# A TensorE order in which an expert tile's routing weights are spread after the down products of the tile two back

## The chip, the core and the metric

The kernel runs on one core of one Trainium2 chip. Its time is the device time of one execution in microseconds (us). The core has five engines that run their own instruction lists and meet at semaphores: TensorE (PE; its weight loads are shown as PEld), VectorE (DVE), ScalarE (ACT), GpSimd (POOL) and SyncE (SP, which only issues transfers here). An engine takes its instructions in the order in which they are written. A wait at the head of the list holds everything behind it.

## The reference, cut to what matters

Two transformer blocks over 2048 tokens of width 256. The change lies in the feed-forward part of block 0, a mixture of experts in which every expert is computed for every token, and the two best are kept by weight:

```python
scores = sigmoid(xf @ gate_w.T)                      # 8 experts
topk_w, topk_idx = top_k(scores, 2)
topk_w = topk_w / (topk_w.sum(-1, keepdims=True) + 1e-20) * 2.5
shared_out = (silu(xf @ shared_wg.T) * (xf @ shared_wu.T)) @ shared_wd.T
h = silu(einsum('td,efd->etf', xf, exp_wg)) * einsum('td,efd->etf', xf, exp_wu)
all_out = einsum('etf,edf->etd', h, exp_wd)          # 8 experts of 176 features
routed_out = (topk_w[..., None] * all_out[topk_idx]).sum(1)
x = x + attention(xn) + shared_out + routed_out
```

Block 1 has 16 causal attention heads and a dense feed-forward layer of 2048 features, whose weights come as 4-bit codes with scales. They are decoded while block 0 runs, on VectorE, ScalarE and GpSimd.

## The kernel before, in words

Tokens lie on the free axis. Block 0 takes them in G = 4 groups of 512 (loop over g). The hidden features of a group are cut into T0 = 14 tiles of 128: tiles t = 0 to 2 are the shared expert (ST = 3), tiles t = 3 to 13 hold the 8 experts' 1408 features side by side (XT = 11). The tile's number over all groups is n = 14 g + t. A product is made in single precision from a high and a low part of each operand, as three matmuls (`prod`, L415 to L417).

For each tile the steps are, with their semaphores:

- **PE `gate_up(t)`**: 12 matmuls of 512 columns into two of the four `ring` banks (s_gu). It waits for s_h of tile t-2, whose banks it takes again.
- **PE spread (L506)**, expert tiles only: one matmul of `sel` and `wT` that copies each expert's routing weights over that expert's rows, into the single bank `pv` (s_wbc). It waits for s_hw of the tile before, that is until VectorE has read `pv`.
- **PE `down0(g, t-2)`**: 6 matmuls that add the tile two back into `acc`. It waits for s_hl of that tile.
- **ACT `activate` (L893)**: SiLU of the gate bank (s_act). **DVE `gated` (L1291)**: times the up bank (s_h). **DVE routed multiply (L1377)**: times `pv` (s_hw), after a wait for s_wbc of this tile. **ACT `split_h` (L903)**: high part `hh`; in ScalarE's order it stands behind the activation of the next tile. **POOL `split_h` (L1125)**: low part `hl` (s_hl).

The order on PE is written out by hand: `gate_up(t)` with the spread at its end, then `down0(g, t-2)`, then the next group's layer norm mean behind t = 4 and its variance behind t = 7 (`ln_mean`, `ln_var`, L424 and L430).

The decoding of block 1's weights goes through the same lists. Steps k = 0 to 25 are placed at tiles n = 8 to 46, two of every three (`step_at`). Step k is, on VectorE behind the routed multiply of its tile: wait for ScalarE's `gval`, L1269, L1272 (two reads from SBUF), then L1280, L1282, L1285 that make the bits of the next value. On ScalarE behind the split of the tile before: `w4h` (L883, waits for GpSimd's `wf` of the step before) and `gval` (L886, waits for L1285 of this step). On GpSimd behind the split: `w4l` (L1125) and `wf` (L1148).

Of the kernel before, what the change touches and what calls it, by code (L numbers as in the profile page):

```python
# [84 lines left out]
def transformer_blocks(nc, xT, w0, gateT, wa, turn_w, biasc, biasv, cols, spread_c, bo, ones_c, sel_c, ident_c, identb_c,  # L85
                       mask_c, tie_c, q4, s4, x1s, w4s, out):
    ctx = ExitStack()
    with ctx:
# [224 lines left out]
        def _(sp):  # L313
# [3 lines left out]
            for n, (src, _, _) in enumerate(pieces):  # L317
                if n >= NS:
                    sp.wait_ge(s_wlo[n % 2], lo_of[n % 2].index(n - NS) + 1)
                sp.dma_start(staged(n), src).then_inc(s_stage[n % NS], 16)  # L320
                if n == 1:
                    sp.wait_ge(s_x, 16)
                    sp.dma_start(xg(1), xT[:, :, NT:2 * NT]).then_inc(s_x, 16)
# [87 lines left out]
        def _(pe):  # L411
            def prod(o, lo_hi_w, x_hi, x_lo, first, last):

                w_hi, w_lo = lo_hi_w
                pe.matmul(o, w_hi, x_hi, start=first, stop=False, skip_group_check=True)  # L415
                pe.matmul(o, w_lo, x_hi, start=False, stop=False, skip_group_check=True)  # L416
                return pe.matmul(o, w_hi, x_lo, start=False, stop=last, skip_group_check=True)  # L417

            def ln_mean(n):
                pe.wait_ge(s_x, 16 * (n + 1))  # L420
                if n > G:
                    pe.wait_ge(s_vb, 2 * (n - G))
                for k in range(KD):
                    mm = pe.matmul(ln_bank(n)[:, :], ones[:, :], xg(n)[:, k, :], start=k == 0, stop=k == KD - 1)  # L424
                mm.then_inc(s_mean, 1)

            def ln_var(n):
                pe.wait_ge(s_sq, n + 1)
                for k in range(KD):
                    mm = pe.matmul(ln_bank(n)[:, :], ones[:, :], sq[:, k, :], start=k == 0, stop=k == KD - 1)  # L430
                mm.then_inc(s_var, 1)

            def normed(n):
                pe.wait_ge(s_xl, n + 1)
                pe.wait_ge(s_xh, n + 1)

            def w(off, width, k, a, b):
                s = w0k(off, width, k, a, b)
                return wh[:, s], wl[:, s]

            def down(tile_no, off, kt, rows, last, first=False):

                pe.wait_ge(s_hl, tile_no + 1)
                th, tl = h_parts(tile_no)
                for m in range(KD):
                    s = w0k(off, D, kt, m * P, (m + 1) * P)
                    mm = prod(acc[:, m, :], (wh[0:rows, s], wl[0:rows, s]), th[0:rows, :], tl[0:rows, :],
                              first, last)
                mm.then_inc(s_dn, 1)

            def down0(g, u):
                down(g * T0 + u, O_SD if u < ST else O_ED, u if u < ST else u - ST, ST_M[u] if u < ST else P,
                     u == T0 - 1)

            pe.wait_ge(s_const, 64)
            for g in range(G):
                if g == 0:
                    ln_mean(0)
                    ln_var(0)
                normed(g)  # L460
                if g == 0:
                    pe.wait_ge(s_wlo[0], 1)
                    pe.wait_ge(s_wlo[1], 1)
                    pe.wait_ge(s_prep, SETUP0)
                else:
                    pe.wait_ge(s_h, T0 * g)
                for m in range(KD):
                    for j, (which, bank, s) in enumerate(((2, (0, 3), s_v), (1, (1, 0), s_k), (0, (2, 1), s_q))):
                        if m == 1 and j == 1:
                            pe.wait_ge(s_vs, 2 * g + 1)  # L470
                        if m == 1 and j == 2:
                            pe.wait_ge(s_kv, 2 * g + 1)
                        if g and m == 0 and j == 1:
                            down0(g - 1, T0 - 1)
                        for k in range(KD):
                            mm = prod(ring[bank[m]][:, :], w(O_QKVO + which * KD * D, D, k, m * P, (m + 1) * P),
                                      xh[:, k, :], xl[:, k, :], k == 0, k == KD - 1)
                        mm.then_inc(s, 1)

                for k in range(KD):  # L480
                    mm = prod(pm[0:N_EXP, :], (gw[:, 0, k, :], gw[:, 1, k, :]), xh[:, k, :], xl[:, k, :],
                              k == 0, k == KD - 1)
                mm.then_inc(s_lg, 1)
                def gate_up(t):
                    n = g * T0 + t
                    if t >= 2:
                        pe.wait_ge(s_h, n - 1)
                    else:
                        pe.wait_ge(s_vh, 2 * g + 2)
                    rows = ST_M[t] if t < ST else P  # L490
                    for o, off, eoff in ((2 * (t % 2), O_SG, O_EG), (2 * (t % 2) + 1, O_SU, O_EU)):
                        for k in range(KD):
                            if t < ST:
                                ww = w(off, SH_FF, k, t * P, t * P + rows)
                            else:
                                ww = w(eoff, XT * P, k, (t - ST) * P, (t - ST + 1) * P)
                            mm = prod(ring[o][0:rows, :], ww, xh[:, k, :], xl[:, k, :], k == 0, k == KD - 1)
                    mm.then_inc(s_gu, 1)
                    if t >= ST:
                        e = g * XT + t - ST  # L500
                        if t == ST:
                            pe.wait_ge(s_wtl, g + 1)
                            pe.wait_ge(s_rk, 11 * g + 1)
                        if e >= 1:
                            pe.wait_ge(s_hw, e)
                        pe.matmul(pv[:, :], sel[:, (t - ST) * P:(t - ST + 1) * P], wT[:, :], start=True,  # L506
                                  stop=True).then_inc(s_wbc, 1)


                if g == 0:  # L510
                    pe.wait_ge(s_wlo[0], 2)
                    pe.wait_ge(s_wlo[1], 2)
                gate_up(0)
                pe.wait_ge(s_sig, g + 1)
                for t in range(4):
                    mm = pe.transpose(pv[:, t * N_EXP:(t + 1) * N_EXP], sig[:, t * P:(t + 1) * P],
                                      identf[0:N_EXP, 0:N_EXP])
                mm.then_inc(s_st, 1)

                pe.wait_ge(s_vhl, 2 * g + 2)  # L520
                if g >= 1:
                    pe.wait_ge(s_res, g)
                for m in range(KD):
                    for k in range(KD):
                        mm = prod(acc[:, m, :], w(O_QKVO + 3 * KD * D, D, k, m * P, (m + 1) * P),
                                  vhh[:, k, :], vhl[:, k, :], k == 0, False)
                mm.then_inc(s_oproj, 1)
                pe.wait_ge(s_rk, 11 * (g + 1))
                for t in range(4):
                    mm = pe.transpose(pm[0:N_EXP, t * P:(t + 1) * P], rwn[:, t, :], identf[:, :])  # L530
                mm.then_inc(s_wt, 1)

                for t in range(1, T0):
                    if g == 0 and t == ST:
                        pe.wait_ge(s_wlo[0], 5)
                        pe.wait_ge(s_wlo[1], 5)
                        pe.wait_ge(s_whi, SEL_PIECE + 1)
                    gate_up(t)
                    if t >= 2:
                        down0(g, t - 2)  # L540
                    if t == LN_AT:
                        ln_mean(g + 1)
                    if t == LN_AT + 3:
                        ln_var(g + 1)
                down0(g, T0 - 2)
# [1190 lines left out]
```

## Time and profile before

| | |
|---|---|
| runs shown | 962.33, 960.31, 960.57 us; median 960.57 us |
| profiled execution | 962.32 us, of it 959.9 us from the first to the last instruction |
| granted TensorE clock, mean | 0.968 of full |
| PE / DVE / ACT / POOL busy | 812.6 / 570.2 / 443.5 / 355.9 us |
| PE waits of the spread (L506) for the routed multiply | 15.3 us in 10 |
| PE waits of down products for POOL's `hl` | 24.4 us in 11 |

A timeline row gives start, duration, engine, line, operation, output from inputs, how many were merged, and in brackets how long the engine had been idle and what ended that. A row of the chain of waits gives start, duration and what held the end at that time. Matmuls are pipelined: one of 512 columns follows the last after 0.23 us at full clock and 0.43 us at half clock, though its own row shows some 0.40 us from start to end.

### The profile page before, as it was taken

The page shows a single profiled execution, that of the slowest core. Times are in us where ns is not written, and L with a number is a line of the kernel's source. Part 1 is how long each engine was busy: PE and PEld are TensorE (multiplying, and loading weights), DVE is VectorE, ACT ScalarE, POOL GpSimd, SP SyncE. Part 2 cuts the span into 40 slices and gives each one's busy share as a digit, 9 for nine tenths or more (in the row PEclk, how much of TensorE's full clock was granted, in tenths as well). Part 3 has the DMA queues.
Part 4 walks back from the last instruction along what each step waited for, and adds up shares of the span by engine and source line. Part 5 has one row for each costly group of instructions (what it writes and reads, how often), then busy time and mean ns, then how long its engine had stood idle before and what let it go on. Part 6 is the DMA issues. An engine that isn't in the chain of part 4 may idle for free.

```text
span 959.9 us, 12682 instructions
## 1 busy us (share of the span) xinstructions
PE 812.6 (85%) x4756; PEld 608.0 (63%) x4756; DVE 570.2 (59%) x919; ACT 443.5 (46%) x687; POOL 355.9 (37%) x277
## 2 busy tenths in 40 slices
PE   3779977895987888998889889889799898898886
PEld 0557755664665666776667667666577576676664
DVE  4742766777687954354556475565656564764735
ACT  3442433343335223434373664564744727645554
POOL 2332332555064614234143333251512434333432
PEclk9979989997999889999899999999999999999999
DMA  6320021332223312537111003020021110020200
GB/s 201 120 86 33 11 88 55 99 88 81 74 77 88 88 55 67 215 141 277 44 35 33 1 23 88 2 67 2 1 77 34 34 35 1 23 67 7 62 1 23
DMA packets 62172, 62.48 MB, mean 65 GB/s; under 512 B 6176, under 2 KB 52128, under 8 KB 61344
## 3 DMA queue, kind: packets, MB, share of 16 engines
q1 hardware_dynamic: 59680, 58.37, 19.7%
q10 hardware_dynamic: 2432, 3.32, 1.1%
q8 instruction: 37, 0.61, 0.3%
q14 instruction: 23, 0.19, 0.1%
HBM read 32.18 MB, written 16.78 MB: 51 GB/s over the span
## 4 chain that ended last, share of the span: by engine, by line
PE 42%; DVE 25%; ACT 16%; issue 10%; DMA 3%; POOL 2%; SPq 1%; ACTq 0%; DVEq 0%; POOLq 0%
PE ring L415 4%; PE ring L416 4%; PE ring L417 4%; DVE gval L1272 3%; PE acc L415 3%; PE acc L416 3%; PE acc L417 3%; DVE gval L1269 3%; ACT act L1024 3%; PE pm L415 2%; ACT L1024 2%; ACT ex L1024 2%; DVE hf L1291 2%; DVE fbits L1280 2%; PE pm L417 2%
## 5 line engine op out<-in xcount | busy, mean ns | idle before, releaser
L1125 POOL TENSOR_TENSOR hl<-hf,hh 128x512 fp32r<-128x512 f32 (+1 forms) x120 | 159.6, 1330 | 462.3 <-ACT hh L903 460.9
L415 PE MATMUL ring<-xh,wh 128*128 128x512 f32 (+1 forms) x272 | 117.1, 431 | 21.1 <-DVE xl L1222 18.5
L415 PE MATMUL acc<-hh,wh 128*128 128x512 f32 (+1 forms) x240 | 104.1, 434 | 24.4 <-POOL hl L1125 24.4
L903 ACT ACTIVATE hh<-hf 128x512 fp32r<-128x512 f32 (+1 forms) x120 | 75.2, 627 | 93.1 <-DVE hf L1397 86.0
L416 PE MATMUL ring<-xh,wl 128*128 128x512 f32 (+1 forms) x272 | 111.4, 410 | 0.0
L417 PE MATMUL ring<-xl,wh 128*128 128x512 f32 (+1 forms) x272 | 110.8, 407 | 0.0
L416 PE MATMUL acc<-hh,wl 128*128 128x512 f32 (+1 forms) x240 | 98.6, 411 | 0.0
L417 PE MATMUL acc<-hl,wh 128*128 128x512 f32 (+1 forms) x240 | 98.5, 410 | 0.0
L1291 DVE TENSOR_TENSOR hf<-act,ring 128x512 f32<-128x512 f32 (+1 forms) x56 | 38.3, 684 | 88.2 <-ACT act L893 83.5
L415 PEld LDWEIGHTS ring<-xh,wh 128*128 128x128 f32 (+1 forms) x272 | 53.8, 198 | 43.0 <-DVE xl L1222 21.6
L657 PE MATMUL ring<-qT,kT 98*128 98x256 bf16 (+1 forms) x256 | 45.6, 249 | 39.6 <-ACT ex L1024 20.3
L415 PEld LDWEIGHTS acc<-hh,wh 128*128 128x128 f32 (+1 forms) x240 | 46.9, 196 | 41.3 <-POOL hl L1125 32.7
L1481 DVE TENSOR_REDUCE mx<-ring 128x2 f32<-128x512 f32 (+1 forms) x96 | 61.8, 684 | 18.8 <-PE ring L630 18.7
L1397 DVE TENSOR_TENSOR hf<-hf,pv 128x512 f32<-128x512 f32 x64 | 43.6, 681 | 45.4 <-PE pv L417 45.1
L1006 ACT ACTIVATE hf<-pm 128x512 f32<-128x512 f32 x64 | 38.1, 596 | 59.2 <-PE pm L417 52.1
L416 PEld LDWEIGHTS ring<-xh,wl 128*128 128x128 f32 (+1 forms) x272 | 53.7, 198 | 14.5 <-issue 1.9
L657 PEld LDWEIGHTS ring<-qT,kT 98*128 98x128 bf16 x256 | 24.2, 98 | 60.6 <-ACT act L1024 29.5
L417 PEld LDWEIGHTS ring<-xl,wh 128*128 128x128 f32 (+1 forms) x272 | 53.1, 195 | 13.7
L893 ACT ACTIVATE act<-ring 128x512 f32<-128x512 f32 (+1 forms) x56 | 33.0, 589 | 52.5 <-PE ring L417 52.4
L415 PE MATMUL pm<-xh,wh 128*128 128x512 f32 x128 | 56.3, 440 | 0.0
L1194 POOL TENSOR_TENSOR pl<-ex,ph 128x512 f16<-128x512 f32 x32 | 40.0, 1252 | 41.4 <-ACT ph L1029 35.7
L1194 POOL TENSOR_TENSOR pl<-act,ph 128x512 f16<-128x512 f32 x32 | 37.2, 1162 | 48.8 <-ACT ph L1029 43.0
(196 smaller groups left out, 1997.4 us busy)
## 6 DMA issues: line engine op xcount, KB each, us to landing
w4s<-w4h SPq DMA_DIRECT2D x24, 256.0 KB, 2.3
w4s<-w4l SPq DMA_DIRECT2D x24, 256.0 KB, 2.8
qT<-qp SPq DMA_DIRECT2D x96, 64.0 KB, 2.6
kT<-kp SPq DMA_DIRECT2D x96, 64.0 KB, 2.7
stage<-w SPq DMA_DIRECT2D x6, 704.0 KB, 4.2
wh<-w4s SPq DMA_DIRECT2D x2, 2048.0 KB, 9.6
wl<-w4s SPq DMA_DIRECT2D x2, 2048.0 KB, 14.4
words<-q SPq DMA_DIRECT2D x12, 256.0 KB, 3.1
```

What stands on the lines that cost most here:

```text
L415: pe.matmul(o, w_hi, x_hi, start=first, stop=False, skip_group_check=True)
L416: pe.matmul(o, w_lo, x_hi, start=False, stop=False, skip_group_check=True)
L417: return pe.matmul(o, w_hi, x_lo, start=False, stop=last, skip_group_check=True)
L657: pe.matmul(o, kT[0:SLOT + 2, h, kt * P:(kt + 1) * P], qT[0:SLOT + 2, h, kt * P:SEQ], start=True, stop=False, skip_group_check=True)
L903: a.activation(h_parts(n)[0][0:rows, :], hf[0:rows, n % 2, :], ACT.Copy).then_inc(s_hh, 1)
L1006: a.activation(hf[:, n % 2, :], pm[:, :], ACT.Gelu_apprx_tanh).then_inc(s_act, 1)
L1024: a.activation(exps(n), ring[f % 2][:, :], ACT.Exp, scale=SCALE).then_inc(s_e, 1)
L1125: return pool.tensor_tensor(dst, src, hi.bitcast(F32), ALU.subtract)
L1194: pool.tensor_tensor(pl[:, n % NP, :], exps(n), ph[:, n % NP, :], ALU.subtract).then_inc(s_plp, 1)
L1291: v.tensor_tensor(hf[0:rows, n % 2, :], act[0:rows, n % 2, :], bank[0:rows, :], ALU.mult).then_inc(s_h, 1)
L1397: v.tensor_tensor(hf[:, n % 2, :], hf[:, n % 2, :], pv[:, :], ALU.mult).then_inc(s_h, 1)
L1481: v.tensor_reduce(mx[:, i, h0:h0 + nh], ring[j % 2][:, :].rearrange("p (n k) -> p n k", n=nh), AX.X, ALU.max).then_inc(s_mx, 1)
```

## The change

The spread becomes a function of its own, `spread_route(t)`, that is called behind `down0(g, t - 2)` and not at the end of `gate_up(t)`. Its waits (s_wtl and s_rk at t = 3, s_hw of the tile before) move with it. `ln_mean` and `ln_var` stay behind all of it. Nothing else is changed: no instruction is added or removed, and no transfer is touched.

```diff
@@ -496,6 +496,7 @@
                             mm = prod(ring[o][0:rows, :], ww, xh[:, k, :], xl[:, k, :], k == 0, k == KD - 1)
                     mm.then_inc(s_gu, 1)
+                def spread_route(t):
                     if t >= ST:
                         e = g * XT + t - ST
                         if t == ST:
@@ -538,6 +539,7 @@
                     gate_up(t)
                     if t >= 2:
                         down0(g, t - 2)
+                    spread_route(t)
                     if t == LN_AT:
                         ln_mean(g + 1)
```

## Rows read from the trace of the kernel before

**Rows 1.** The page's busy times, and its chain that ended last, by engine.
```profile
PE 812.6 (85%) x4756; PEld 608.0 (63%) x4756; DVE 570.2 (59%) x919; ACT 443.5 (46%) x687; POOL 355.9 (37%) x277
PE 42%; DVE 25%; ACT 16%; issue 10%; DMA 3%; POOL 2%; SPq 1%; ACTq 0%; DVEq 0%; POOLq 0%
```

**Rows 2.** Who waited for whom: total us, times, longest us.
```profile
PE acc L415 <- POOL hl L1125: 24.4, 11, 5.3
...
PE pv L506 <- DVE hf L1377: 15.3, 10, 4.7
```

**Rows 3.** Windows: stretch, length, then busy us of PE, PEld, DVE, ACT, POOL, clock, DMA.
```profile
311.00:318.00 7.00, 6.17 (x15) 4.79 (x16) 6.79 (x9) 1.61 (x3) 5.41 (x4) 0.51 0.40 114
...
376.00:423.00 47.00, 47.00 (x197) 36.54 (x196) 18.91 (x26) 15.11 (x24) 16.65 (x13) 1.00 0.34 121
```

**Rows 4.** Timeline around the spread of tile t = 4, group 2, with decoding step 16.
```profile
273.90 1.27 POOL L1125 TENSOR_TENSOR hl<-hf,hh 96x512 fp32r<-96x512 f32 x1 [2.83 <-ACT hh L903]
...
274.81 0.50 PE L506 MATMUL pv<-wT,sel 128*128 128x512 f32 x1 [2.60 <-DVE hf L1377]
...
275.23 0.50 PE L415 MATMUL acc<-hh,wh 96*128 96x512 f32 x1
...
276.00 0.69 DVE L1377 TENSOR_TENSOR hf<-hf,pv 128x512 f32<-128x512 f32 x1
276.02 0.40 PE L415 MATMUL acc<-hh,wh 96*128 96x512 f32 x1
276.59 1.26 POOL L1148 TENSOR_TENSOR wf<-gval,scl 128x512 f32<-128x512 f32 x1 [0.17 <-POOL w4l L1125]
276.61 1.80 DVE L1269 SCALAR_TENSOR_TENSOR gval<-fbits,gval 128x512 f32<-128x512 f32 x1
277.81 1.74 POOL L1125 TENSOR_TENSOR hl<-hf,hh 128x512 fp32r<-128x512 f32 x1
...
278.44 1.66 DVE L1272 TENSOR_TENSOR gval<-gval,sbits 128x512 uint32<-128x512 uint32 x1
```

**Rows 5.** Timeline: the same two VectorE operations while GpSimd is idle.
```profile
364.42 0.68 DVE L1269 SCALAR_TENSOR_TENSOR gval<-fbits,gval 128x512 f32<-128x512 f32 x1
365.14 0.69 DVE L1272 TENSOR_TENSOR gval<-gval,sbits 128x512 uint32<-128x512 uint32 x1
```

**Rows 6.** Timeline: tile t = 7, group 0, where TensorE never waits.
```profile
89.59 0.40 PE L506 MATMUL pv<-wT,sel 128*128 128x512 f32 x1
...
91.14 0.69 DVE L1377 TENSOR_TENSOR hf<-hf,pv 128x512 f32<-128x512 f32 x1
```

**Rows 7.** Timeline: tile t = 11 of group 0, then t = 12 of group 1.
```profile
112.59 0.69 DVE L1377 TENSOR_TENSOR hf<-hf,pv 128x512 f32<-128x512 f32 x1
...
220.30 0.69 DVE L1377 TENSOR_TENSOR hf<-hf,pv 128x512 f32<-128x512 f32 x1
220.78 0.63 PE L415 MATMUL acc<-hh,wh 128*128 128x512 f32 x1
221.92 1.74 POOL L1125 TENSOR_TENSOR hl<-hf,hh 128x512 fp32r<-128x512 f32 x1
```

**Rows 8.** Timeline: tiles t = 10 and 11 of group 2.
```profile
312.43 0.63 PE L415 MATMUL acc<-hh,wh 128*128 128x512 f32 x1
313.22 0.69 DVE L1377 TENSOR_TENSOR hf<-hf,pv 128x512 f32<-128x512 f32 x1
...
319.37 0.60 ACT L893 ACTIVATE act<-ring 128x512 f32<-128x512 f32 x1 [0.25 <-PE ring L417]
...
320.73 0.69 DVE L1377 TENSOR_TENSOR hf<-hf,pv 128x512 f32<-128x512 f32 x1
```

**Rows 9.** Timeline: the first expert tile's turn in group 0.
```profile
68.75 0.72 PE L415 MATMUL acc<-hh,wh 128*128 128x512 f32 x1 [3.59 <-POOL hl L1125]
```

**Rows 10.** Chain that ended last, around decoding step 16 (start, us, what held the end).
```profile
276.69 1.72 DVE gval L1269
...
278.44 1.67 DVE gval L1272
```

## The prediction

> **What bounds the kernel now.** The page first: TensorE is busy 812.6 us of 959.9, and the chain that ended last runs over it for 42% only, over VectorE for 25% and ScalarE for 16% [rows 1]. So no engine bounds the whole. Next, the list of waits. The spread (L506) held TensorE up 10 times for 15.3 us, always for the routed multiply of the tile before; the down products held it up 11 times for 24.4 us, for GpSimd's `hl` [rows 2]. The change puts the second wait ahead of the first, so the question is which of the two ends last. Then the windows, which show two regimes in block 0: from 376 to 423 us, decoding over, TensorE is busy 47.00 of 47.00 us [rows 3] and a tile takes 12 + 1 + 6 matmuls of 0.23 us, 4.4 us; in the decoding, tiles n = 8 to 46, TensorE waits. Last, the chain in that part: routed multiply, L1269, L1272, bits, ScalarE's `gval`, next activation, gated, routed again [rows 10]. It is a loop through VectorE, and the operation that the change delays stands in it. Everything from 432 us on is outside the change.
>
> **The waits that go.** All ten waits of the spread look like the one at 274.81 [rows 4]. TensorE stood 2.60 us until VectorE had read `pv`, started the spread at 274.81 and the down products at 275.23. But `hl`, for which those wait, was itself only done at 273.90 + 1.27 = 275.17. Both waits hang on one activation of ScalarE: gated and routed multiply take 2 x 0.69 us after it, high part and low part 0.63 + 1.27 and the hand-overs, some 0.5 us more. In each of the ten `hl` comes after the spread could start, so the down products start where they did. Gain: 0. The stall is given over in full to L1125.
>
> **What is added on TensorE.** In such a tile the spread ran in the shadow of the wait for `hl`. Behind the down products it has no shadow: `gate_up(t+1)` starts one matmul later, 0.23 us. That counts only where TensorE's chain sets the end behind it: t = 3 of group 0, where the down products started at 68.75 after a 3.59 us wait [rows 9], t = 3 of group 3 (one more of the kind), and t = 10 of group 2, counted below. 2 x 0.23 = 0.46 us. In tiles without a wait, order does not change TensorE's sum. No queue but TensorE's is reordered, and no DMA moves.
>
> **What is delayed on VectorE.** The routed multiply waits for the spread, which is now 6 matmuls later, 1.4 us.
> In an undisturbed tile the spread starts at 89.59 and the multiply at 91.14 [rows 6]; the new spread starts at 89.59 + 6 x 0.23 = 90.98, ends 0.40 later at 91.4, and the multiply comes 0.25 us late. Who waits for it? The high part, which stands behind the next activation, 4 us off: cost 0. These are 14 of 44 tiles. At t = 3 of groups 0 and 3 it is 2.9 and 0.8 us late, before the same long gap and with no decoding step behind it that VectorE works on: 0. In most of the decoding's other tiles VectorE reaches the multiply 0.6 to 6 us after the new spread is done: 0. Two (t = 5 and 8 of group 2) have 0.1 us to spare.
> What is left are pairs of tiles that follow each other fast, because the first has no decoding step and the second has. In the example [rows 4] the down products end with 276.02 + 3 x 0.23 = 276.7, the spread at 277.12, and the multiply starts at 277.14 for 276.00, 1.14 us late. Six such tiles: t = 11 in group 0 (112.59 becomes 113.57, +0.98), t = 3, 6 and 12 in group 1 (+1.14, +0.64, and +2.2, where TensorE runs at half clock [rows 7]), t = 4 and 7 in group 2 (+1.14, +1.15). Sum 7.25 us. At t = 10 of group 2 the multiply is 2.2 us late, but there the next activation waited for TensorE [rows 8], so of that 1.35 us reaches t = 11. With the 0.46 us this would be **9.1 us, if every delay went through**.
>
> **Why most of it does not.** Behind the multiply stand L1269 and L1272, which take 0.62 and 0.69 us while GpSimd is idle [rows 5] (0.62 without the hand-over that its row of 0.68 holds) and 1.72 and 1.67 us here [rows 10]. Their ends fit one reading: GpSimd's `wf` ends at 276.59 + 1.26 = 277.85, L1269 ends 0.56 later at 278.41; then `hl`, begun at 277.81, takes 1.74 for its usual 1.27 and ends at 279.55, and L1272 ends 0.56 later at 280.11. Each waits for the other's instruction to be over. So VectorE stands 1.1 us before L1269 anyway, and a multiply that is 1.14 us late falls into that wait: L1269 would be issued at 277.83, just before `wf` ends. If it still goes ahead of `hl`: 0. If `hl` goes first: `hl` to 279.13, L1269 to 279.69, L1272 free of it to 280.39, for 280.11: +0.28. The same by hand for the others: t = 11 group 0 +0.22, t = 3 group 1 +0.23, t = 6 0, t = 12 (`hl` begun at 221.92 runs to 223.2, then both free [rows 7]) +0.28, t = 7 group 2 0 or +0.28. At t = 10 and 11 of group 2: the activation at 319.37 comes 0.23 later through TensorE, the multiply at 320.73 becomes 321.46 [rows 8], and the waits for GpSimd leave +0.61 in all. Sum: 0.22 + 0.23 + 0 + 0.28 + 0.61 = 1.34, with the two open ones 1.34 to 1.9, with TensorE's 0.46 **1.8 to 2.4 us; I take 2.1**.
> The Trainium skill (SBUF — State Buffer, "SBUF: two separate sides") says of the port pair that VectorE and GpSimd share that it is an exclusive lock, which whoever starts first holds for the whole instruction. By that the sum is the 2.1 us; were the two merely slowed down together it would be the 9.1. The trace agrees: the 0.56 us twice.
>
> The profiled execution's own time, 962.3 us, becomes 964.4. It lies 1.75 us above the median of the runs, 960.57 us, and the median becomes 960.6 + 2.1 = **962.7 us**.
>
> **Rivals.**
> 1. **Delays go through** (9.1 us, 969.7): GpSimd's operations would have to shift with VectorE. Against it: `wf` and `hl` [rows 4] hang on values of the tile before, long done. Chance 0.12.
> 2. **A new half-clock spell at t = 4 of group 2.** TensorE stands 2.6 us there and 3.0 us after the change, since the spread no longer breaks the pause; a pause of 4.75 us went with a clock of 0.51 [rows 3, 8], one of 2.6 did not. At half clock the down products take 1.2 us more, `gate_up(5)` 0.5; activation and multiply of t = 5 have 0.6 and 0.1 us to spare: +1.6 us, 964.3. The Trainium skill (TensorE: Matmul & The Clock Gate, "HAM oscillation") says that pauses bring half clock back, which speaks against the change; the trace agrees [rows 8]. Chance 0.13.
> 3. **All of it drowns** (0 to 1.4 us, 960.6 to 962.0): L1269 wins each tie, and in the 0.23 us places something else is late. Chance 0.18.
> 4. **Faster: VectorE and GpSimd fall out of step.** L1272 takes 1.67 us where it meets GpSimd and 0.69 where not [rows 5, 10]. Shifted by some 0.3 us, later meetings may fall out otherwise: from three steps on that lose one each, 3 x 0.98 = 2.9 us, more than the 2.1: 959.8; five give 957.8. Against: after each place VectorE, ScalarE and GpSimd shift together. Chance 0.07.
>
> **How the numbers follow.** The forecast has 0.50. About 0.2% (1.9 us) is what a measurement of this kernel can tell from none, so slower begins at 962.5, faster below 958.6. The forecast's 962.4 to 963.3 lies mostly above: 0.33 of its 0.50, which with rivals 1 and 2 makes 0.58 for slower. Same is the other 0.17, rival 3 and 0.01 of rival 4, 0.36; faster the rest of rival 4, 0.06. The range leaves out rival 1's full size and the faster end: 960.2 to 967.5; its upper part holds rival 2 twice over and delays that go through in half of the places.
>
> **What would show it.** The waits of the spread for L1377 gone from 15.3 to under 3 us; those of the down products for L1125 up by 12 to 18 us. In six to seven tiles a wait of VectorE at L1377 for TensorE of 0.6 to 2.2 us, some 8 us in all, and behind it shorter L1269 and L1272: their means over 100 to 338 us, together, down by some 0.2 us. The span from 62 to 432 us longer by 1.8 to 2.4 us, the rest the same. Wrong, if the spread still waits after the down products, if `hl` is done earlier and TensorE gains, or if L1269 begins late and still takes 1.7 us.

## The result and the profile after

Over 19 runs each, side by side, the changed kernel takes 964.54 us (median) and the kernel before 962.02 us: a ratio of 1.0027, 95% interval 1.0018 to 1.0036, or 2.6 us with 1.7 to 3.5 us. It is slower, and the 2.1 us of the forecast lie inside that interval. The median of before, 962.02 us, lies 1.5 us above the 960.57 us of the three runs shown first, on which the forecast's 962.7 us rested.

The page of the kernel after, busy times and chain, against [rows 1]:

```profile
PE 807.7 (84%) x4756; PEld 605.9 (63%) x4756; DVE 562.3 (58%) x919; ACT 443.3 (46%) x687; POOL 352.6 (37%) x277
PE 43%; DVE 22%; ACT 16%; issue 11%; DMA 3%; POOL 3%; SPq 1%; ACTq 0%; DVEq 0%; POOLq 0%
```

Who waited for whom in it (total us, times, longest), against [rows 2]:

```profile
PE acc L415 <- POOL hl L1127: 43.5, 21, 5.4
...
DVE hf L1379 <- PE pv L507: 19.4, 24, 2.7
```

TensorE's wait in the spread for the routed multiply, 15.3 us, is gone from the list. The wait of the down products for `hl` rose by 19.1 us, from 24.4: the same pauses under the other name, ten places more. Nine of the spread's ten pauses are among them; the tenth, 0.24 us at t = 9 of group 1, shows in `after_again`. New is the second line: VectorE stood 24 times for the spread. (Lines behind the new function are numbered 1 or 2 higher: L507 is the spread, L1271 and L1274 are L1269 and L1272 of before.)

The timeline around the spread of tile t = 4, group 2, the place of [rows 4]. Everything is 0.83 us later here than before, a shift from earlier tiles:

```profile
276.05 0.50 PE L415 MATMUL acc<-hh,wh 96*128 96x512 f32 x1 [2.77 <-POOL hl L1127]
...
277.56 0.40 PE L507 MATMUL pv<-wT,sel 128*128 128x512 f32 x1
278.06 0.69 DVE L1379 TENSOR_TENSOR hf<-hf,pv 128x512 f32<-128x512 f32 x1 [1.27 <-PE pv L507]
278.65 1.28 POOL L1127 TENSOR_TENSOR hl<-hf,hh 128x512 fp32r<-128x512 f32 x1
278.67 1.80 DVE L1271 SCALAR_TENSOR_TENSOR gval<-fbits,gval 128x512 f32<-128x512 f32 x1
...
280.50 0.69 DVE L1274 TENSOR_TENSOR gval<-gval,sbits 128x512 uint32<-128x512 uint32 x1
```

The down products start with no gain (275.23 + 0.83 = 276.06). The multiply comes at 278.06 for 276.83, 1.23 us late. `hl`, whose row begins at 278.65, goes first, runs its undisturbed 1.28 us (before: 1.74). L1271 begins late and still takes 1.80 us, because it waits for `hl` now and not for `wf`; L1274 is free, 0.69 us for 1.66. The last ends 0.26 us late instead of 1.23. The chain that ended last runs through exactly these:

```profile
277.72 0.25 PE pv L507
...
278.06 0.69 DVE hf L1379
278.75 1.73 DVE gval L1271
...
280.50 0.70 DVE gval L1274
```

Read tile by tile, as the start of ScalarE's activation after the place minus the same before it, both against the kernel before:

```
place (group, tile)    multiply late by   passed on   forecast
(0,11)                 1.06               0.30        0.22
(1,3)                  1.23               0.34        0.23
(1,6)                  0.73 (*)           0.26 (**)   0
(1,12)                 1.87               0.28        0.28
(2,4)                  1.23               0.26        0 or 0.28
(2,7)                  1.23               0.28        0 or 0.28
(2,10), with (2,11)    2.49               0.24        0.61
(3,3), TensorE         -                  0.26        0.23
(0,3), TensorE         -                  1.39 (***)  0.23
14 undisturbed tiles   0.35               0           0
(*) against the activation of tile 5: that of tile 6 itself came 0.53 us sooner here, at no gain
(**) 0.08 in after_again, see there
(***) some 0.2 of it at the same clock, see below
```

The seven places pass on 1.97 us of some 10 us of lateness. Outside these nine the setup was 1.35 us shorter in this profile than in that of before, and the openings of groups 1, 2 and 3 shifted by -0.9, +0.4 and -0.1 us. In the opening of group 1 it is the half-clock stretch that is shorter (8 matmuls of the long spacing for 14). The same -0.9 us came in `after_again` and in only_rest, but not in only_seven, so that it may belong to the order; this is not shown.

### The profile page after: what moved, and what is told of

Same layout as the page of the kernel before. It is cut to its first block, busy times and chain, and to the rows that moved or that the text cites. A ratio compares the mean times of both kernels' runs of the same rounds, so it can differ in the third digit from the quotient of the medians.

```text
span 961.7 us, 12682 instructions
## 1 busy us (share of the span) xinstructions
PE 807.7 (84%) x4756; PEld 605.9 (63%) x4756; DVE 562.3 (58%) x919; ACT 443.3 (46%) x687; POOL 352.6 (37%) x277
## 4 chain that ended last, share of the span: by engine, by line
PE 43%; DVE 22%; ACT 16%; issue 11%; DMA 3%; POOL 3%; SPq 1%; ACTq 0%; DVEq 0%; POOLq 0%
PE acc L415 4%; PE ring L415 4%; PE ring L417 4%; PE ring L416 4%; PE acc L416 3%; PE acc L417 3%; DVE gval L1274 3%; ACT act L1026 3%; POOL hl L1127 2%; DVE gval L1271 2%; ACT L1026 2%; ACT ex L1026 2%; PE pm L415 2%; DVE hf L1399 2%; PE pm L416 2%
## 5 line engine op out<-in xcount | busy, mean ns | idle before, releaser
L1127 POOL TENSOR_TENSOR hl<-hf,hh 128x512 fp32r<-128x512 f32 (+1 forms) x120 | 157.0, 1308 | 468.1 <-ACT hh L905 466.7
```

What stands on the lines that cost most here:

```text
L1127: return pool.tensor_tensor(dst, src, hi.bitcast(F32), ALU.subtract)
```

## The experiments

The theory: in seven places a multiply comes late and VectorE's waits for GpSimd swallow most of it; two more places cost TensorE one matmul. Rivals: the other 37 tiles add up; the small price per place is simply TensorE's extra matmul; the delays pass through and something else gives back.

**Which tiles pay.** Seven alone, then the other 37 alone (the edit is against the kernel after):

```diff
+FAST = {(0, 11), (1, 3), (1, 6), (1, 12), (2, 4), (2, 7), (2, 10)}
...
                     gate_up(t)
+                    behind = (g, t) in FAST        # only_rest: not in FAST
+                    if not behind:
+                        spread_route(t)
                     if t >= 2:
                         down0(g, t - 2)
-                    spread_route(t)
+                    if behind:
+                        spread_route(t)
```

> The spread is moved behind the down products in seven tiles alone, (group, tile) = (0,11), (1,3), (1,6), (1,12), (2,4), (2,7), (2,10), those where a decoding tile follows fast on one without a step. Theory (seven late multiplies, each mostly swallowed by VectorE's wait for GpSimd): +1.9 us (7 x 0.27), ratio 1.002; in the trace each of the seven adds 0.25 to 0.3 us to the activation after it. Rival (the other 37 spreads add up, since their multiplies come 0.35 us late): 0, ratio 1.000.

Measured: 964.66 us for 962.20 of before, ratio 1.0028 (1.0016 to 1.0041), 2.7 us. Four places pass on what they do in the whole change (0.30 us at (0,11), 0.33 at (1,3), 0.29 at (2,7), 0.24 at (2,10)), and (1,6) passes on 0.08. At (1,12) and (2,4) TensorE fell to half clock in this profile (granted clock 0.50 from 220 to 222 and from 278 to 280 us), the multiply came 2.50 and 2.69 us late, and the next activation 0.68 and 2.76 us. VectorE waited for the spread 7 times, 12.2 us.

> The spread is moved behind the down products in the other 37 expert tiles, and stays in front in the seven. Theory: +0.5 us (t = 3 of groups 0 and 3, 0.23 us each, through TensorE), ratio 1.0005, and no shift of the activations at the seven. Rival (the other 37 add up): +2 us, ratio 1.002.

Measured: 963.03 us, ratio 1.0008 (0.9993 to 1.0022). No activation behind the seven is shifted by the move; the shifts seen there, 2.4 us at (2,4) and -0.4 us at (2,10), come where TensorE's half-clock stretches changed (the first is shown further down). So the 14 multiplies that come 0.35 us late cost nothing, and the seven carry the greater part. The shares (2.7 and 0.8 us) are each uncertain by over 1 us; the tile table is the sharper reading.

**Is it swallowed, and how much can be?** VectorE alone is delayed, with TensorE's order as before: one, three or five reductions ahead of the gated multiply in the seven tiles.

```diff
             def gated(n, bank, rows):
                 ...
+                for i in range(K if divmod(n, T0) in FAST else 0):     # K = 1, 3, 5
+                    j = K * sorted(FAST).index(divmod(n, T0)) + i
+                    v.tensor_reduce(spare[0:rows, j:j + 1], bank[0:rows, :], AX.X, ALU.add)
```

> The order of before; in the seven tiles VectorE does one extra reduction of the up bank (about 0.68 us) ahead of the gated multiply, so that the routed multiply comes 0.7 us late without a change on TensorE. Theory (VectorE stands some 1.1 us for GpSimd's instruction at L1269 in most of them): 0 to 0.2 us in a place, together 0 to +1.5 us. Rival (delays go through): 7 x 0.69 = +4.8 us.

> The same with three reductions, 2.07 us late. Theory: L1269 is issued behind hl's start, hl runs on undisturbed, L1269 and L1272 (1.66 us before) both run free behind it: about +0.3 us where GpSimd is busy twice, +0.3 to +1.3 us in the two or three places with less waiting, together +2 to +5 us. Rival (delays go through): +14.5 us.

> As late_3, with five reductions, 3.4 us late. Theory: past the end of GpSimd's second instruction VectorE has no wait left to hide in, and each further 0.69 us comes through in full: 1.4 us more than late_3 in each of the seven places, in the time +8 to +12 us. Rival (the places have other slack, which still hides it): under +5 us.

Measured: 0.5 us (ratio 1.0005, 0.9991 to 1.0019), 2.8 us (1.0029, 1.0017 to 1.0041) and 10.2 us (1.0106, 1.0079 to 1.0133). In the traces the multiply comes 0.59, 1.79 and 2.98 us late, and the seven places pass on 0.2, 3.0 and 8.7 us together (at (2,4) and (2,10), where TensorE or its clock sets the next activation, the end of VectorE's decoding step is taken). The place (2,7) in the three timelines; first one reduction:

```profile
297.70 1.27 POOL L1150 TENSOR_TENSOR wf<-gval,scl 128x512 f32<-128x512 f32 x1 [0.17 <-POOL w4l L1127]
297.72 0.69 DVE L1382 TENSOR_TENSOR hf<-hf,pv 128x512 f32<-128x512 f32 x1
298.33 1.19 DVE L1271 SCALAR_TENSOR_TENSOR gval<-fbits,gval 128x512 f32<-128x512 f32 x1
298.94 1.73 POOL L1127 TENSOR_TENSOR hl<-hf,hh 128x512 fp32r<-128x512 f32 x1
299.55 1.66 DVE L1274 TENSOR_TENSOR gval<-gval,sbits 128x512 uint32<-128x512 uint32 x1
```

Three:

```profile
298.36 1.28 POOL L1127 TENSOR_TENSOR hl<-hf,hh 128x512 fp32r<-128x512 f32 x1
298.94 1.25 DVE L1271 SCALAR_TENSOR_TENSOR gval<-fbits,gval 128x512 f32<-128x512 f32 x1
300.23 0.69 DVE L1274 TENSOR_TENSOR gval<-gval,sbits 128x512 uint32<-128x512 uint32 x1
```

Five:

```profile
304.98 1.29 POOL L1127 TENSOR_TENSOR hl<-hf,hh 128x512 fp32r<-128x512 f32 x1
...
306.76 0.69 DVE L1271 SCALAR_TENSOR_TENSOR gval<-fbits,gval 128x512 f32<-128x512 f32 x1
307.48 0.69 DVE L1274 TENSOR_TENSOR gval<-gval,sbits 128x512 uint32<-128x512 uint32 x1
```

Before the change L1269 took 1.80 us and L1272 1.66 here. With a delay of 0.60 us L1269 still gets its turn between `wf` and `hl`: shorter by the delay, 0 passed on. With 1.79 us `hl` is ahead, and 0.27 us is passed on. With 2.99 us both run free, and 0.91 us comes through. The change's 1.23 us lies on the same step as 1.79 us does: 0.28 us. That rules out TensorE's extra matmul as the cause of the 0.27, though the two sizes are near each other: `late_3` has no extra matmul. From late_3 to late_5 a place passes on 0.8 us more in the mean, where 1.4 were expected: a reduction delays by 0.60 us, not 0.68, and at 1.79 us some of the hiding place was still unused.

How much can be hidden in a place can be read from the profile of the kernel before: it is what the operations behind the multiply take beyond their free 0.68, 0.69 and 0.43 us. At (2,7) that is (1.80 - 0.69) + (1.66 - 0.69) = 2.08 us, and 2.99 - 2.08 = 0.91 us. The same sum in all seven, with the durations from the kernel before and what late_5 (2.98 us late) passed on:

```
place     L1269  L1272  L1280   to hide in   2.98 less that   measured
(0,11)    1.44   0.69   0.43    0.76         2.22             2.23
(1,3)     0.68   1.66   1.33    1.87         1.11             1.11
(1,6)     1.33   1.67   0.43    1.63         1.35             1.36
(1,12)    1.60   1.67   0.43    1.89         1.09             1.09
(2,4)     1.80   1.66   0.43    2.08         0.90             0.90
(2,7)     1.80   1.66   0.43    2.08         0.90             0.91
(2,10)    1.61   1.66   0.43    1.89         1.09             1.09
```

It holds for the change too where the delay exceeds the place: 1.06 - 0.76 = 0.30 us at (0,11), as measured, and 2.49 - 1.89 = 0.60 us for the end of the decoding step at (2,10). Of that 0.26 us reach the next activation, since before the change that one had waited for TensorE. Below that size a place passes on 0 to 0.34 us (once 0.60, at (1,3) in late_3), depending on whose turn it is. At (1,3) a third operation, L1280, has its share in the waiting.

**Without GpSimd's reads.** Its three kinds of instructions in block 0 become memsets (the low parts of h from tile 3 on and the decoded weights are left out), with either order:

```diff
+                if 2 < n < T0 * G:
+                    pool.memset(tl[0:rows, :].bitcast(F32), 0.0).then_inc(s_hl, 1)
+                    return
                 low(tl[0:rows, :], hf[0:rows, n % 2, :], th[0:rows, :]).then_inc(s_hl, 1)
...
-                    low(w4l[:, k % 2, :], wf[:, :], w4h[:, k % 2, :]).then_inc(s_w4l, 1)
+                    pool.memset(w4l[:, k % 2, :].bitcast(F32), 0.0).then_inc(s_w4l, 1)
...
-                    pool.tensor_tensor(wf[:, :], gval[:, (k - 1) % 2, :], scl[:, :], ALU.mult).then_inc(s_w, 1)
+                    pool.memset(wf[:, :], 0.0).then_inc(s_w, 1)
```

> The order of before; in block 0's tile loop GpSimd's three kinds of instructions (hl from tile 3 on, w4l, wf) are memsets that read nothing, so the low parts of h, and the decoded weights of block 1, are left out. Theory: L1269 and L1272 take 0.62 to 0.70 us in all 24 steps; the kernel is faster by 10 to 30 us, since some 30 us of VectorE's time in them was waiting for GpSimd.

> The same memsets with the order of after. Theory: with nothing to hide in, the late multiplies go through: in the fast tiles that remain 0.7 to 1.2 us each, +4 to +8 us against free_port_before. Rival (the wait for GpSimd had nothing to do with it): the same +2.6 us as between the two whole kernels.

Measured: 925.22 and 929.53 us for 963.23 of the kernel before, 38 us less (10 to 30 were expected) and 34 us less; between them 4.3 us. The groups by line of free_port_before, 100 to 310 us (busy, mean ns, then idle before):

```profile
L1275 DVE TENSOR_TENSOR gval<-gval,sbits 128x512 uint32<-128x512 uint32 x22 | 15.2, 692 | 0.8
L1272 DVE SCALAR_TENSOR_TENSOR gval<-fbits,gval 128x512 f32<-128x512 f32 x22 | 15.1, 684 | 0.0
```

All 22 of each take the free time; in the kernel before they take 1442 and 1282 ns in the mean over 100 to 338 us. That the waiting is for GpSimd's reads is shown, and not for its being busy: the memsets, 0.53 us each, overlap these instructions 32 times in free_port_before (that of `wf` overlaps L1272 at 117.45 us by 0.33 us), and none of the 48 takes over 0.70 us. That the delays pass through is shown only in the small: the memset ends 0.75 us sooner than `hl`, the down products start sooner, and the multiply in most places is just 0.35 us late. Where VectorE's loop sets the pace the whole 0.35 is passed on ((1,3): 0.35), elsewhere TensorE's pace hides it. Much of the 4.3 us is half-clock stretches, as at (0,3) below (1.4 us of it); the pair doesn't settle the 0.7 to 1.2 us that were expected per place.

**Is the multiply worth moving at all?** VectorE's decoding step ahead of the routed multiply, with three orders on TensorE: of before, of after, and with the spread one tile later.

```diff
+                    dequant(step_at(n))
                     if t >= ST:
                         ...
                         v.tensor_tensor(hf[:, n % 2, :], hf[:, n % 2, :], pv[:, :], ALU.mult).then_inc(s_hw, 1)
-                    dequant(step_at(n))
```

> The order of before on TensorE; VectorE does its decoding step ahead of the routed multiply and not behind it. Theory (the multiply's 0.69 us stand in VectorE's loop in every decoding step, and the value is not needed before the high part that stands behind the next activation): up to 24 x 0.7 = 16 us less; but the spread of the next tile waits for this multiply, now up to 5 us later, ahead of the down products, and takes part of it back: -4 to -12 us. Rival (a new wait takes it all): 0 or slower.

> Decoding step ahead of the routed multiply, with the order of after. The spread's wait for the late multiply stands behind the down products but still ahead of gate_up of the next tile, so most of decode_first_before's loss stays: +8 to +14 us against before. Rival (the down products between take it up): +0 to +5 us.

Measured: 974.37 us for 963.23 (ratio 1.0121, 1.0093 to 1.0148) and 964.99 us for 961.98 (1.0025, 1.0010 to 1.0041). Both theories failed, and the rivals named with them came in. TensorE's waits, with the order of before:

```profile
PE pv L506 <- DVE hf L1378: 32.2, 15, 4.4
```

and with the order of after:

```profile
PE acc L415 <- POOL hl L1127: 29.6, 15, 3.9
...
PE pv L507 <- DVE hf L1380: 16.2, 10, 2.9
```

With a multiply that is late on VectorE, the spread in front holds up the down products and the next gate and up products. Behind them that wait is half as long. The one for `hl` grows (18.1 us, then 29.6), but ScalarE's activations wait 66.7 us for their products and not 77.2. So the tested change is worth some 9 us (11.7 less 2.4) in a kernel where the spread's wait outlasts that for `hl`, and costs 2.6 us here, where it doesn't.

The third order, as an edit against the kernel after (VectorE's edit above goes with it):

```diff
                     gate_up(t)
+                    if t > ST:
+                        spread_route(t - 1)
                     if t >= 2:
                         down0(g, t - 2)
-                    spread_route(t)
...
+                spread_route(T0 - 1)
                 down0(g, T0 - 2)
```

> Decoding step ahead of the routed multiply on VectorE, and on TensorE the spread of tile t behind gate_up(t+1), ahead of down0(t-1). Theory: the multiply leaves VectorE's loop (0.7 us in each of some 20 steps), and the spread's wait for the multiply of the tile before, which cost decode_first_before 32.2 us of waiting, finds it long done: 4 to 14 us less than before. Rival (the multiply must wait for gate_up(t+1) in tiles without a step, and the high part behind it is late): between -2 and +5 us.

Measured: 961.90 us for 961.98, ratio 1.0004 (0.9990 to 1.0019). The wait of the spread fell from 32.2 us to 3.4, yet the 4 to 14 us that were expected do not come. VectorE in tile (1,4) of it:

```profile
174.87 0.69 DVE L1295 TENSOR_TENSOR hf<-act,ring 128x512 f32<-128x512 f32 x1 [0.59 <-ACT act L897]
175.47 1.78 DVE L1273 SCALAR_TENSOR_TENSOR gval<-fbits,gval 128x512 f32<-128x512 f32 x1
```

and in the kernel before:

```profile
175.17 0.69 DVE L1377 TENSOR_TENSOR hf<-hf,pv 128x512 f32<-128x512 f32 x1
175.78 1.08 DVE L1269 SCALAR_TENSOR_TENSOR gval<-fbits,gval 128x512 f32<-128x512 f32 x1
```

The operation starts 0.7 us sooner in its tile (0.31 us on the clock of the trace, with the tile itself 0.40 us later) and takes 0.70 us longer. It is the same swallowing from the other side: time taken out ahead of a wait for GpSimd becomes waiting. It is not the whole account. In five tiles the step to the next activation is 0.3 to 0.9 us shorter than before, and the step into group 2 is 2.3 us longer, behind a multiply at (1,13) that comes 6.2 us late; the rival of the expectation, late multiplies in tiles without a decoding step, is not ruled out for that part.

**The changed kernel once more.**

> The kernel after, unchanged. The same small shifts at the same nine tiles, 0.2 to 0.35 us each, and no other shift outside stretches at half clock; whether t = 4 of group 2 falls to half clock is open, as it did in only_rest, late_1 and late_3, which have the order of before there. Time +1.7 to +3.5 us.

Measured: 964.82 us for 961.98, ratio 1.0035 (1.0020 to 1.0051). Against the first profile its activations keep one distance to within 0.02 us from one tile to the next, but for a few steps of up to 0.2 us. Eight of the nine steps are the same. The ninth, (1,6), passes on 0.08 us here and 0.26 in the first profile, and it shows a tie from both sides. In the first profile:

```profile
186.44 1.30 POOL L1127 TENSOR_TENSOR hl<-hf,hh 128x512 fp32r<-128x512 f32 x1
186.44 1.84 DVE L1271 SCALAR_TENSOR_TENSOR gval<-fbits,gval 128x512 f32<-128x512 f32 x1
188.32 0.69 DVE L1274 TENSOR_TENSOR gval<-gval,sbits 128x512 uint32<-128x512 uint32 x1
```

and in `after_again`:

```profile
184.70 0.69 DVE L1271 SCALAR_TENSOR_TENSOR gval<-fbits,gval 128x512 f32<-128x512 f32 x1
184.71 1.83 POOL L1127 TENSOR_TENSOR hl<-hf,hh 128x512 fp32r<-128x512 f32 x1
185.42 1.67 DVE L1274 TENSOR_TENSOR gval<-gval,sbits 128x512 uint32<-128x512 uint32 x1
```

One order of the two instructions costs 0.26 us and the other 0.08, in the same kernel.

**A version that beats both.** If the turns with GpSimd are the price, move GpSimd. Its decoding pair waits until VectorE has made its bits, and so runs while VectorE waits or takes one of its inputs from PSUM (the multiply at 274.07 us of the kernel before takes its usual 0.69 us beside an `hl`):

```diff
                 for t in range(T0):
+                    if step_at(g * T0 + t) > 0:
+                        pool.wait_ge(s_bits, 3 * min(step_at(g * T0 + t) + 1, 2 * NQ))
+                    dequant(step_at(g * T0 + t))
                     split_h(g * T0 + t, ST_M[t] if t < ST else P)
                     if g == 0 and t < 2:
                         weights((9, SEL_PIECE + 1)[t])
-                    dequant(step_at(g * T0 + t))
```

> The order of before on TensorE and VectorE. On GpSimd the decoding pair (w4l, wf) of a tile stands ahead of that tile's hl and waits until VectorE has made the bits of its step (L1285). Theory (the two engines take turns at L1269, L1272 and L1280, some 2.3 us in a step): w4l and wf now run while VectorE stands or works from PSUM, only hl is left to meet L1269: about 1 us less in each of 15 or more steps, 5 to 20 us less than before, with L1272 near 0.7 us in most steps. Rival (the waiting moves to ScalarE's w4h or to hl, which the down products wait for): between -4 us and slower.

Measured: 948.27 us for 962.03, ratio 0.9863 (0.9839 to 0.9886): 13 us less than before the change, on TensorE's old order. Groups by line, 100 to 330 us:

```profile
L1274 DVE TENSOR_TENSOR gval<-gval,sbits 128x512 uint32<-128x512 uint32 x22 | 22.0, 999 | 0.8
L1271 DVE SCALAR_TENSOR_TENSOR gval<-fbits,gval 128x512 f32<-128x512 f32 x22 | 21.4, 974 | 0.0
L1282 DVE TENSOR_SCALAR fbits<-words 128x512 uint32<-128x512 uint32 x22 | 10.3, 467 | 2.3
```

The three took 1442, 1282 and 841 ns in the mean before. ScalarE's wait for `wf` fell too (75.1 to 10.8 us). How the 13 us divide between the two is not shown.

## Why the prediction was right, and where it was off

- **The waits that go: right.** The pauses were taken over by `hl`, and the down products started no sooner, but for 0.18 us at (2,10), where the spread had run at half clock. The spread's waits are 0 where under 3 us were named; the waits for `hl` rose by 19.1 us where 12 to 18 were named.
- **The late multiplies: right in place, nearly in size.** Six named at 0.64 to 2.2 us were 0.73 to 1.87 us late, (2,10) 2.49 for 2.2. VectorE's wait for TensorE was 10.1 us in the seven, not some 8, and 19.4 us in all: the undisturbed tiles' 0.35 us (0.25 forecast) count in it, and so does the 2.7 us at t = 3 of group 0, both at no cost.
- **The swallowing: right, and shown.** L1269 and L1272 together lost 0.31 us a step in the mean (1282 to 1189 and 1442 to 1220 ns), 6.9 us in 22 steps, where some 0.2 us were named. The dose at (2,7) gives 0, then a step of 0.27 us, then the excess over 2.08. The Trainium skill (SBUF — State Buffer, "SBUF: two separate sides") calls the port pair that VectorE and GpSimd share an exclusive lock, held for a whole instruction; the dose and the table of the seven places agree. Rival 1 (9.1 us) is out. The two open ties went to `hl` in both profiles of after.
- **A sign that was drawn wrong.** "L1269 begins late and still takes 1.7 us" was to speak against the prediction. At (2,4) and (2,7) it takes 1.80 and 1.81 us, and yet the delay is swallowed. The prediction's own second case (`hl` to 279.13, L1269 to 279.69) has it so: when `hl` goes first, L1269 stays long and L1272 is free. The span between the activations of t = 3 in group 0 and t = 13 in group 3 is 2.90 us longer where 1.8 to 2.4 were named, the 1.2 us of a change of clock at (0,3) among it. The "962.4 to 963.3" of the chances is a slip: the sum gives 962.4 to 963.0.
- **Terms mis-sized, with some luck in the sum.** (2,10) with (2,11) was 0.24 us, not 0.61: the second meeting with GpSimd passed on nothing. Its first part was right by number only: the activation of t = 11 comes 0.26 us later (0.23 named), but through VectorE, whose decoding step ends 0.61 us late, and not through TensorE, for which ScalarE no longer waits there. (1,6) was 0.26 and 0.08 us, not 0, a tie that falls either way. (0,11) and (1,3) were 0.1 us higher. These errors nearly cancel. The seven places and (3,3) come to 2.2 us; the forecast's terms for them are 1.6 to 2.1.
- **TensorE's term at (0,3): right within a mode, and the modes not foreseen.** The step from activation 3 to 4 in group 0 is 1.39 us longer in this profile, for 0.23. The windows of the kernel before and then of after (the third column from the end is the granted clock):

```profile
67.00:70.00 3.00, 1.25 (x3) 1.07 (x4) 1.55 (x3) 1.35 (x3) 2.57 (x2) 0.81 0.00 0
70.00:73.00 3.00, 3.00 (x10) 2.31 (x10) 0.21 (x1) 0.00 (x0) 1.99 (x2) 0.62 0.35 98
```
```profile
67.00:70.00 3.00, 2.46 (x6) 1.98 (x7) 0.69 (x1) 0.15 (x1) 3.00 (x3) 0.50 0.00 0
70.00:73.00 3.00, 3.00 (x9) 2.32 (x8) 0.69 (x1) 0.00 (x0) 0.77 (x1) 0.50 0.74 240
```

  In the one the half-clock stretch (1.2 for 2.4 GHz) ends within the down products and `gate_up(4)`, in the other it covers more of them. Over all profiles the step comes in two lengths. With the spread ahead of the down products it is 7.39 to 7.54 us in six and 8.64 and 8.77 us in two; with the spread behind them 7.75 us in one and 8.87 to 8.97 us in four. Within a length the change costs 0.2 us, as forecast; a change of length costs 1.2 us. TensorE's pause ahead of it is 3.6 us in the profile of before and 4.1 us in that of after, so rival 2's mechanism may make the long one likelier here, at another tile than I named. The pauses of all fourteen profiles bear on that: the eight short steps, spread_next's 7.53 us among them, stand behind pauses of 2.24 to 3.93 us, the six long ones behind 3.88 to 4.15 us, and the new order had the longer pauses (3.93 to 4.15 us, for 2.24 to 3.90). Whether the timed runs of after hold more long steps than those of before was not measured, and so it stays open how much of the 2.6 us comes from here.
- **Rival 2 at (2,4)** did not occur in either profile of after. The pause it leans on is this one of the kernel before, ahead of (2,10):

```profile
311.83 0.80 PE L506 MATMUL pv<-wT,sel 128*128 128x512 f32 x1 [4.75 <-DVE hf L1377]
```

  Half clock came at (2,4) in kernels of either order (only_seven has the new one there); only_rest, with the old order at that tile, has

```profile
274.00:278.00 4.00, 4.00 (x9) 2.48 (x8) 3.93 (x4) 0.63 (x1) 3.79 (x3) 0.50 0.56 149
```

  That stretch is a matter of the run. With 0.23 us at (0,3) the nine places come to 2.5 us, and 2.6 us were measured. The closeness proves little: the opening of group 1 (-0.9 us) and the two lengths at (0,3) are each of some 1 us and lie outside that sum.

## What to carry to other kernels

Where a wait is removed, ask which wait ends next and whether both hang on the same event: here `hl` ended 0.4 us behind the multiply, and reordering gained nothing while it took the spread out of a pause. A delay ahead of an instruction that waits for another engine anyway is worth only what it exceeds that wait by, and a saving ahead of it can turn into waiting; the late_1 kernel and tile (1,4) of spread_next are the two sides of it. The lever is then the other engine's schedule: moving two GpSimd instructions out of VectorE's way gave 13 us, where the four reorderings of TensorE and VectorE that were tried gave none. How much a delay can hide is the sum of what the instructions behind it take beyond their free durations.

## What the hardware showed that was not expected

- L1269 and L1272 took 29.6 us more in 22 steps than they take without GpSimd's reads (1282 and 1442 ns for 684 and 692), by taking turns; with L1280 (841 ns for 427) it is 38.7 us. In a trace it shows only as the spread of one instruction's duration (L1272: 0.69 or 1.66 us), never as idle time.
- Two traces of the same kernel agree to 0.02 us in most steps from tile to tile over 330 us. So steps of 0.25 us can be read from one profile, while 19 timed runs resolve 0.9 us. The exceptions are ties, as at (1,6), and stretches at half clock.
